# Expert tiles in two passes of fifteen, the first begun before the second half's rows are scattered

## The reference, cut to what matters

```python
x = x + tanh(g_xattn) * attention(layernorm(x), ctx)
scores = softmax(layernorm(x) @ gate_w + gate_b)      # 8 experts, the two best are kept in wf
out = 0
for i in range(8):
    wi = wf[:, i:i + 1]
    y = relu(xf * wi @ w1[i] + b1[i]) @ w2[i] + b2[i]   # 128 -> 512 -> 128
    out = where(wi > 0, y, out)
x = x + tanh(g_ffn) * out
```

## Time and profile before

| | us |
|---|---|
| median of 3 runs | 188.35 (188.20 to 189.06) |
| the profiled execution, its own time | 188.17 |
| its span, first to last instruction | 186.1 |
| TensorE busy in it | 136.0 (73%) |
| VectorE busy in it | 120.7 (65%) |
| ScalarE busy in it | 90.3 (49%) |
| GpSimd busy in it | 91.0 (49%) |
| mean granted TensorE clock | 0.843 of full |

### The profile page before, as it was taken

How to read it: one execution, slowest core, us unless ns; L and a number is a source line. 1 busy time by engine, 2 the same in 40 slices (tenths; PEclk the granted TensorE clock), 3 DMA queues, 4 the chain that set the end, 5 groups by cost and what they waited for, 6 DMA issues and landing times.

```text
span 186.1 us, 5245 instructions
## 1 busy us (share of the span) xinstructions
PE 136.0 (73%) x1685; PEld 109.1 (59%) x1685; DVE 120.7 (65%) x380; ACT 90.3 (49%) x208; POOL 91.0 (49%) x133
## 2 busy tenths in 40 slices
PE   7489786999988989989683501000999999999930
PEld 2074444678666767667452300000999999999930
DVE  5585848546689989999774778510266667576520
ACT  1277770015587887787781100002466676576300
POOL 8384899743264540604107376760034455455460
PEclk9858999555799999999999655555599999999995
DMA  4965976754024034544410002521112222221100
GB/s 121 264 203 158 241 198 170 207 150 108 21 61 121 7 130 137 195 138 152 161 41 30 30 15 64 164 62 41 50 43 58 65 59 54 72 65 55 30 0 0
DMA packets 17992, 18.34 MB, mean 99 GB/s; under 512 B 2944, under 2 KB 15747, under 8 KB 17952
## 3 DMA queue, kind: packets, MB, share of 16 engines
q1 hardware_dynamic: 15104, 14.50, 27.6%
q0 software_dynamic: 1280, 2.25, 3.9%
q10 hardware_dynamic: 1584, 1.29, 2.6%
HBM read 8.80 MB, written 3.26 MB: 65 GB/s over the span
## 4 chain that ended last, share of the span: by engine, by line
PE 52%; DVE 10%; POOL 9%; ACT 9%; issue 7%; DMA 6%; another core or an unknown queue 2%; ACTq 1%; SPq 1%; DVEq 0%; POOLq 0%
PE pair L1157 12%; POOL rows_dram L517 6%; PE bank L1167 6%; PE pair L1167 6%; PE bank L1071 5%; ACT probs L654 4%; DMA value_pack<-in_value 4%; PE pair L1043 4%; PE pair L1056 3%; PE bank L1117 3%; PE pair L987 3%; DVE smax L798 2%; PE pair L1028 2%; DVE routed L783 2%
## 5 line engine op out<-in xcount | busy, mean ns | idle before, releaser
L798 DVE TENSOR_REDUCE smax<-pair 128x8 f32<-128x1024 f32 x32 | 39.5, 1309 | 7.3 <-PE pair L1056 7.2
L565 POOL DMA_INDIRECT out<-ctxT,tokens x23 | 23.4, 1019 | 33.1 <-DVE ctxT L963 18.6
L654 ACT ACTIVATE probs<-pair 128x1024 f32<-128x1024 f32 x32 | 32.5, 1015 | 11.5 <-PE pair L1043 11.5
L1157 PE MATMUL pair<-ctxT,q_stack 128*128 128x128 f32 x184 | 25.9, 287 | 0.0
L1157 PEld LDWEIGHTS pair<-ctxT,q_stack 128*128 128x128 f32 x184 | 24.0, 204 | 0.0
L517 POOL DMA_INDIRECT rows_dram<-routed,rowpos x16 | 15.9, 994 | 14.2 <-DVE routed L897 9.1
L956 DVE TENSOR_SCALAR q_stack<-pair,q_stack 128x128 f32<-128x128 f32 x46 | 13.9, 344 | 12.6 <-PE pair L1157 12.6
L700 ACT ACTIVATE q_stack<-pair,q_stack 128x128 f32<-128x128 f32 x46 | 14.4, 365 | 15.4 <-PE pair L1157 15.4
L690 ACT ACTIVATE q_stack<-q_stack 128x128 f32<-128x128 f32 x23 | 11.3, 492 | 20.3 <-DMA q_stack<-rows_dram 19.9
L1149 PE MATMUL pair<-first_pack,q_stack 128*128 128x128 f32 x23 | 6.8, 294 | 17.2 <-ACT q_stack L690 16.4
L1071 PE MATMUL bank<-probs,vall 128*18 128x128 f32 x512 | 18.0, 283 | 0.6 <-ACT probs L654 0.6
(11 more groups left out here) (167 smaller groups left out, 277.0 us busy)
## 6 DMA issues: line engine op xcount, KB each, us to landing
wexp<-in_wexp SPq DMA_DIRECT2D x8, 514.0 KB, 3.4
k_stack<-k_part SPq DMA_DIRECT2D x24, 128.0 KB, 2.7
q_stack<-q_part SPq DMA_DIRECT2D x24, 128.0 KB, 2.9
q_stack<-rows_dram SPq DMA_DIRECT2D x23, 68.5 KB
x<-in_x SPq DMA_DIRECT2D x4, 256.0 KB, 7.4
ctxT<-in_ctxT SPq DMA_DIRECT2D x3, 256.0 KB, 7.4
out<-ctxT,tokens POOLq DMA_INDIRECT x23
late_pack<-in_late ACTq DMA_DIRECT2D x1, 329.5 KB, 5.2
```

The source lines that it names most:

```text
L565: pool.indirect_dma_start(io["out"], bass.IndirectOffsetOnAxis(ap=tokens[t % R][:, :].bitcast(u32), axis=0), result[t % R], None, bounds_c ...
L654: nc.scalar.activation(probs[s % 2][:, t].rearrange("p h g q -> p (h g q)"), shifted_pair[:, :], ACT.Exp, scale=HD ** -0.5).then_inc(s_exp, 1)
L798: V.reduce_max(smax[q % 2][:, :, CHUNK * t:CHUNK * (t + 1)], score_pair[t][:, :].rearrange("p (h g k) -> p h g k", h=2, g=CHUNK), axis=AX.X)\
L1157: ins = M(out, w1cur[k.u][:, c * P:(c + 1) * P], rowsT[k.u], start=True, stop=True)
```

## The change

The routing of each half becomes complete in itself: own `rows_dram`, own places from zero, own pads, own table. The experts run over 15 tiles of half 0 (8 full ones and at most 7 more), then over 15 tiles of half 1. So 30 tiles are run where 23 were. The table of half 0 is made on VectorE inside attention step 18, the first three w1 copies inside step 19. The table of half 1 is made inside the expert steps 6 and 8. All pads go out on SyncE's queue; those of half 1 stand between the load of tile 5 and the load of tile 6. `row_weights(0)` moves from step 17 to step 16, `scatter` of half 0 is issued in two pieces (3 and 5 DMAs) instead of three (2, 2 and 4), and the expert loops are written out. The eight matmuls by which `rank(1)` counted on from half 0 go.

```diff
-GROUPS = ((0, 8), (8, 16))
+SPLIT = 8
+PASSES = ((0, SPLIT), (SPLIT, SEQS))
...
-CAP = TOKENS + P
-TILES = TOKENS // P + EXPERTS - 1
+CAP = max(end - first for first, end in PASSES) * QLEN + P
+PASS_TILES = tuple(end - first + EXPERTS - 1 for first, end in PASSES)
+TILES = sum(PASS_TILES)
...
-        RANK_STEP = 17
+        RANK_STEP, TABLE_STEP, W1_STEP = 17, 18, 19
+        W1_AHEAD, PADS_TILE, TABLE_TILES = 3, R, (6, 8)
...
+        def pads(eng, g):
+
+            for e in range(EXPERTS):
+                first = eng.value_load(pad_rows[g][0:1, e:e + 1], min_val=0, max_val=EXPERTS * CAP)
+                eng.dma_start(rows_dram[g][ds(first, P), :], spare).then_inc(s_pad[g], 16)
...
             sp.wait_ge(s_padrow, 1)
             pads(sp, 0)
...
+            sp.wait_ge(s_spare, 32)
+            sp.wait_ge(s_s2, HALVES * SEQS)
+
+            def load_tile(n, item):
                 if t := item(0):
...
+                    if t.no == PADS_TILE:
+                        sp.wait_ge(s_padrow, 2)
+                        pads(sp, 1)
+                    if t.place == 0:
+                        sp.wait_ge(s_pad[t.turn], 16 * EXPERTS)
+                        sp.wait_ge(s_tab, t.turn + 1)
+                        first, end = PASSES[t.turn]
+                        sp.wait_ge(s_scat[t.turn], 16 * (end - first))
...
             pool.wait_ge(s_routed, 1)
             pool.wait_ge(s_weight, 1)
-            scatter(0, 2)
+            scatter(0, 0, 3)
             invert_std(2)
-            scatter(2, 4)
+            scatter(0, 3, SPLIT)
             invert_std(LAST)
-            scatter(4, 8)
             pool.wait_ge(s_routed, 2)
             pool.wait_ge(s_weight, 2)
-            scatter(8, SEQS)
+            scatter(1, SPLIT, SEQS)
...
             gate_exp(1)
-            act.wait_ge(s_padrow, 1)
-            pads(act, 1)
...
                 if n == RANK_STEP:
                     row_places(0)
-                    row_weights(0)
                 if n in STATS_STEP:
                     second_stats(STATS_STEP[n])
+                if n == TABLE_STEP:
+                    tile_counts(0)
+                    tile_table(0)
+                elif n == W1_STEP:
+                    dve.wait_ge(s_wexp, 16 * EXPERTS)
+                    dve.wait_ge(s_s2, HALVES * SEQS)
+                    for k in range(W1_AHEAD):
+                        place_w1(k)
                 if n == SEQS:
                     second_choice(0)
+                    row_weights(0)
...
+            def place_w1(no):
+
+                t = Item(no)
+                dve.wait_ge(s_tab, t.turn + 1)
+                e = dve.value_load(tab[t.turn][0:1, t.place:t.place + 1], min_val=0, max_val=EXPERTS - 1)
+                wait(dve, s_down, no - R + 1)
+                wait(dve, s_rv, no - R + 1)
+                V.tensor_copy(w1cur[t.u], wexp[:, ds(e, 1), HC * D:WROW].rearrange("p a w -> p (a w)")).then_inc(s_w1, 1)
...
+                if n >= LAG_UP and n + 1 < TILES:
+                    place_w1(n + 1)
+                if n == TABLE_TILES[0]:
+                    tile_counts(1)
+                elif n == TABLE_TILES[1]:
+                    tile_table(1)
+            experts(expert_step)
...
             attention(one_step)
             pe.wait_ge(s_exp, HALVES * SEQS)
+            pe.wait_ge(s_x1, SEQS)
             rank(1)
 
-            pe.wait_ge(s_tab, 1)
```

More of the change, by code:

```diff
@@ L290, in build, with __init__ @@
         class Item:
[L293 to L313, removed]
+            def __init__(self, no):
+                self.no, self.u, self.lap, self.no2 = no, no % R, no // R, no % 2
+                self.turn = no >= PASS_TILES[0]
+                self.place = no - self.turn * PASS_TILES[0]
         LAG_MT, LAG_S2, LAG_PV, LAG_HT, LAG_OUT = 1, 3, 4, 5, 6
         LAG_TURN, LAG_UP, LAG_DOWN = 1, 2, 3
-        RANK_BANKS = (None, 0)
-        EXPERTS_FIRST = 11
-        assert (TILES - EXPERTS_FIRST) % R == 0 and EXPERTS_FIRST >= LAG_DOWN + R - 1
         def attention(one_step):
@@ L361, in every, with choices @@
             return a.unsqueeze(1).to_broadcast([P, at.stop - at.start, EXPERTS])
+        def choices(g):
+            first, end = PASSES[g]
+            return chosenb[:, first + g:end + g, :]
         def group_ranks(g):
-            first, end = GROUPS[g]
-            width = end - first + (end == SEQS)
-            out = dve_bank[:, 392:] if g == 0 else bank[RANK_BANKS[g]]
-            return out[:, 0:width * EXPERTS].rearrange("p (t e) -> p t e", e=EXPERTS)
+            first, end = PASSES[g]
+            width = end - first + 1
+            return dve_bank[:, 392:392 + width * EXPERTS].rearrange("p (t e) -> p t e", e=EXPERTS)
         block = ctx.enter_context(nc.Block())
@@ L547, in _ @@
                 elif n == 9:
[L548 removed]
+                    for g in range(2):
+                        pool.dma_start(rows_dram[g][EXPERTS * CAP:EXPERTS * CAP + P, :], spare).then_inc(s_spare, 16)
                 elif n == 11:
@@ new lines, in row_places, with tile_counts @@
+                V.tensor_copy(pad_rows[g][:, :], ranks[0:1, end - first, :]).then_inc(s_padrow, 1)
+            def tile_counts(g):
+                order.after(V.tensor_scalar(ntiles_i[:, :], count[:, :], float(P - 1), None, ALU.add))
+                order.after(V.tensor_scalar(ntiles_i[:, :], ntiles_i[:, :], 7, None, ALU.arith_shift_right))
+                order.after(V.tensor_copy(ntiles[:, :], ntiles_i[:, :]))
+                E88 = [P, EXPERTS, EXPERTS]
+                order.after(V.tensor_tensor(tab8[:, :, :], upto, ntiles[:, :].unsqueeze(1).to_broadcast(E88), ALU.mult))
+                V.tensor_scalar(adjust[:, :], ntiles[:, :], -float(P), float(CAP), ALU.mult, ALU.add)
+                order.after(V.reduce_sum(ends[:, :], tab8[:, :, :], axis=AX.X))
```

145 lines of the change are left out of this document (59 added, 86 removed).

## The result

| | before | after |
|---|---|---|
| median, us | 188.27 (186.84 to 189.06, 4 runs) | 200.33 (199.51 to 201.36, 4 runs) |
| profiled execution, its span | 188.17, 186.1 | 199.51, 197.4 |

The ratio is 1.0653, 95% interval [1.0571, 1.0734]. The sign was forecast; the size was not: 193.6 us, and 197.0 at the top of the range.

The account below looks back on a forecast made before the run. TensorE was taken to set the pace, with a hole before the experts. Span 186.1 + (131.6 - 141.43) + 14.0 + 1.2 = 191.5, plus 2.07 outside it: 193.6 us, range 191.0 to 197.0.

Parts of the forecast that it names:

- Later transfers ... No cost.: Expert stage: GpSimd's second scatters, load(15) and result stores were claimed to add no time.
- 4.3: Attention steps 16 to 21: VectorE's added work makes it 4.3 us late, moving rank(1)'s end to about 117.3.
- 3.5 us for the w1 copies: Attention step 19: three w1 copies with register loads take 3.5 us on VectorE, lower bound 2.25.
- VectorE's wait of 2.66 us: Step 19's rsum wait, claimed to absorb most of 0.6 plus 3.5 us for counts and table, leaving 1.4 late.
- The time of tile 6: SyncE's eight pads between tiles 5 and 6: first 119.8, load(6) 129.1, turn(6) 131.6; pads cost 2.4 us.
- The colder stop: Rival at tile 6: half clock costs up to 2.3 us, or slower pads 3.0; time 195.5 to 197; chance 20%.
- Table and counts: Half 1, expert steps 6 and 8: counts hidden by tile 6's wait; table makes TensorE wait 1.2 us, bounds 0 and 2.3.
- The seven more tiles: TensorE expert stage: 30 tiles instead of 23 at 2.005 us each, adding 14.0 us.
- -9.8: The hole before the experts gives back 9.8 us: turn(6) at 131.6 instead of 141.43.

Follow-up runs that it names:

- held occasion: Kernels measured together on one chip, with remote waits in their traces; three of eight occasions, kernel before at 188.27, 187.78 and 189.12 us.
- quiet occasion: Kernels measured together on one chip, without those remote waits; five of eight occasions, kernel before at 185.71, 185.02, 185.45, 185.44 and 185.56 us.
- scatters in fours: Changed kernel, half 1's pads one behind each load of tiles 6 to 13, second scatters in two runs behind results of tiles 0 and 4: 1.0287.
- the kernel without pads: Changed kernel without the eight pads of half 1, its second pass loading half 0's rows again: 1.0522.
- spaced scatters: Changed kernel with half 1's eight scatters one behind each result of tiles 0 to 7: 1.0574, again 1.0579.
- plain stores: Changed kernel with half 1's indirect scatters replaced by eight plain stores to a separate tensor: 1.0596, again 1.0593.
- late scatters: Kernel before, loops written out, with all half 0 scatters behind both deviations: 1.0249.

## Why the prediction was wrong, step by step

**"Later transfers ... No cost."** This step failed. On the occasion of the first measurement ScalarE, VectorE and SyncE were held while the second scatters ran, and TensorE starved. From the last `probs` to `turn(6)` the forecast had 35.0 us (131.6 - 96.57); it took 40.9 (from 95.24) on the held occasion and 34.7 (from 97.22) on the quiet one. So the hold costs 6.2 us. That it needs a held occasion is shown by the changed kernel, which has it on one and not on the other. That it needs these scatters rests on one kernel, the one without them, which took 34.1 us on a held occasion. In the forecast's own terms the first trace is late by 4.6 us at `turn(6)`, 0.5 in tiles 6 and 7, 0.2 at the table and 0.6 behind the last `turn`: 5.9, from a span of 191.5 to 197.4. The median lies 0.8 above that execution.

**The trace of before held the same thing.** ScalarE's 3.3 us in step 18 was on the path to the second choice. Below are that row, from the first trace of before, and then VectorE's `rsum` in the quiet trace of the same program:

```profile
101.19 0.38 ACT L662 ACTIVATE oT<-bank 128x256 f32<-128x256 f32 x1 [3.34 <-remote]
```

```profile
100.76 0.26 DVE L805 RECIPROCAL rsum<-bank 128x16 f32<-128x16 f32 x1 [0.54 <-PE bank L1104]
```

`rank(1)` ends 16.3 us behind the last `probs` (96.57) in the earlier trace rows, and 14.0 in the quiet trace (110.93 and 96.89); in the held trace of before with its loops written out it is 17.0. The prediction never asks about ScalarE's wait. On a held occasion the delay is absorbed in part by it: the change adds 19.4 - 16.3 = 3.1 us there, on a quiet one 19.3 - 14.0 = 5.3. The forecast was 4.3, between the two, and partly by luck. It took 3.5 us for the w1 copies, less 0.63, and they made 1.7. It let VectorE's wait of 2.66 us absorb most of the table, and that wait was the hold's: with 0.54 in its place, 0.6 + 3.5 - 0.54 + 1.7 is the 5.3 of the quiet occasion, and with 2.66 the same sum gives the 3.1 of the held one, if the copies made 1.7 there too. (112.86 + 4.3 is 117.2, not the 117.3 written.)

**The time of tile 6.** Without the hold this chain came out nearly as written: first pad 118.96 (119.8 forecast), `load(6)` 128.88 (129.1), `turn(6)` 131.94 (131.6), in a trace whose last `probs` is 0.65 us later than that of before. What the pads cost there: with pads spread and scatters in fours `turn(6)` is 11.6 us behind `turn(0)`, in the changed kernel 15.5, so 3.9 us where I had 2.4. From the first pad to `load(6)` it took 9.9 us instead of 9.3, as one issue took 1.09 us instead of 0.33; from `load(6)` to `turn(6)` 3.1 instead of 2.5; and TensorE by itself is 0.3 us quicker through tiles 0 to 5 than I took it to be. The Trainium skill, "DMA: Bandwidth & Descriptors", § Issuing engines are not separate DMA queues, calls the saving of a second issuing engine "usually small relative to the DMA itself". Here eight issues in a row took 9.16 us, beside 1.84 us for one load's transfer, so for such a run the rows disagree. No run divided the second pads between two queues, so what a second queue would save was not measured.

**The colder stop.** It was given as a rival at 20%, in place of the forecast; it came on top of it. In the quiet trace of the changed kernel:

```profile
132.00:134.00 2.00, 2.00 (x9) 1.89 (x10) 0.00 (x0) 0.86 (x4) 1.64 (x2) 0.50 0.45 118
134.00:136.00 2.00, 2.00 (x15) 1.99 (x12) 0.74 (x4) 1.03 (x4) 0.00 (x0) 0.66 0.03 5
136.00:138.00 2.00, 2.00 (x20) 1.99 (x19) 1.35 (x7) 1.28 (x5) 0.93 (x1) 1.00 0.16 35
```

Behind 3.29 us without work the clock is at the half level, and tiles 6 and 7 take 5.73 us instead of 4.01: 1.7 us. That is the behaviour which the Trainium skill's "TensorE: Matmul & The Clock Gate", § HAM oscillation, describes, and the trace agrees.

**Table and counts.** The table costs 1.2 us in the quiet trace (`turn(8)` to `turn(12)` 9.24 us instead of 8.02) and 1.4 in the first; forecast 1.2. The counts, hidden by the wait for tile 6 as forecast, show where the pads are spread: tiles 6 and 7 take 4.6 us there.

**The seven more tiles.** `turn(12)` to the last takes 34.09 us for 17 tiles, 2.005 each, in both traces of the changed kernel: 14.0 us for seven, as forecast.

**The sum redone** on one quiet occasion, where the change costs 10.3 us by the medians (195.72 and 185.45) and 5.3 were forecast; both spans are from profiled executions, 183.7 and 194.8. `turn(6)` 139.04 to 131.94: -7.1. Tiles: +14.0. Half clock: +1.7. Table: +1.2. From the last `turn` to the end: 13.8 for 12.6, +1.2, where no forecast had a term; it lies behind the last result's store. Together 11.0, measured 11.1. The forecast had -9.8, +14.0, +1.2. Of the 2.7 us between -7.1 and -9.8 nearly all is that before, without its hold, reaches `turn(6)` 42.2 us behind the last `probs` instead of 44.9.

On the held occasion the same sum (spans 186.1 and 197.4) is -5.3, +14.0, +0.5 for tiles 6 and 7, +1.4 and +0.6: 11.2, measured 11.3. Its `turn(6)` has the hold in it, and its clock had recovered by then (0.92 of full from 136 to 138).

**Still open.** What makes an occasion held, and what inside the chip releases ScalarE and VectorE in one moment: 129.61 is 2.7 us behind the start of the last indirect DMA then queued (126.95), and 130.7 in the kernel without pads is 2.6 behind its 128.05; but with pads spread ScalarE and VectorE were released at 127.99 already, 1.0 behind its 126.97, and once more at 129.5. That the engines lacked their instructions in a hold is not excluded: the profile's page counts the same transfers of instructions in the held and the quiet trace of the changed kernel (16 and 13 packets on two queues), but not for whom they came or when they were asked for. What else ran on the chip is not on record. Whether spaced scatters, plain stores or late scatters avoid a hold was never seen, since all those runs met quiet occasions.

## What to carry to other kernels

Splitting padded work into two halves pays its padding twice: here seven tiles and 14.0 us, against a hole of 16.5 us of which the quiet trace got back 11 at tile 0 and kept 7 at tile 6. A run of register-addressed DMA issues in the middle of a queue is a stop (eight took 9.2 us here). In seven traces TensorE's waits of 1.75 to 3.73 us for tile 6 were each followed by 1.5 to 3.1 us of delay at the half clock within two tiles, and the longer wait didn't always bring the larger loss; count the two as one term. When a variant measured on another occasion removes a wait, run the unchanged kernel beside it and compare a stretch that neither edits, before giving the edit the credit.

## What the hardware showed that was not expected

The same program on the same input has or lacks waits of 2 to 7 us that no work in the trace ends, depending on the occasion. Among the tiles ScalarE, VectorE and SyncE have them together; in attention step 18 ScalarE waits 3.3 us while VectorE runs on. All profiled kernels of an occasion agree; of the other executions only the time is known. The kernel before differs by 2 to 4 us between the two (185.0 to 185.7 against 187.8 to 189.1), the changed one by 4.6 (195.72 and 200.33). In all traces that have them they lie where GpSimd has indirect stores under way, and GpSimd itself isn't slowed: its stores take 0.96 us each, 0.30 apart, on either occasion.
